# A two-layer gated cross-attention and mixture kernel: two of four probability tiles turned by VectorE and transfers, and plain steps in another order

## The reference

```python
x = x + tanh(g_xattn[0]) * L0_xattn(layernorm(x), ctx)
x = x + tanh(g_ffn[0])   * L0_ffn(layernorm(x))       # linear layer with weights from 4 bit planes
x = x + tanh(g_xattn[1]) * L1_xattn(layernorm(x), ctx) # 16 heads of 128
x = x + tanh(g_ffn[1])   * L1_ffn(layernorm(x))       # 16 experts, top 4, first batch's 512 rows only
...
q = rmsnorm(hidden @ Wq, gq); k = rmsnorm(enc @ Wk, gk); v = enc @ Wv
attn = softmax(q @ k.T * scale)
out  = (attn @ v) @ Wo
```

## Time and profile before

| | us |
|---|---|
| median of 3 runs | 1463.31 |
| fastest and slowest run | 1462.25, 1465.47 |
| span of the profiled execution | 1461.5 |
| PE busy | 1437.8 |
| DVE busy | 1107.0 |
| ACT busy | 977.5 |
| POOL busy | 864.5 |

### The profile page before, as it was taken

The page is one execution under the profiler, slowest core; times in us unless marked ns, Lnnn a source line. Parts: engine busy times, 40 slices in busy tenths (PEclk is TensorE's granted clock), DMA queues, the critical chain, the costliest instruction groups (busy, mean ns, idle before and its releaser), DMA issues.

```text
span 1461.5 us, 23763 instructions
## 1 busy us (share of the span) xinstructions
PE 1437.8 (98%) x8086; PEld 1223.0 (84%) x8086; DVE 1107.0 (76%) x2100; ACT 977.5 (67%) x2224; POOL 864.5 (59%) x701
## 2 busy tenths in 40 slices
PE   8999999999999999999999999999999999999998
PEld 6778788888888888888888888888888888888887
DVE  7888777777777777777777777777777776787777
ACT  7864477777776667667676767667676765666664
POOL 4785555555554566666575757575666655664341
PEclk9999999999999999999999999999999999999999
DMA  8420011111111333434333433433434331321002
GB/s 325 159 66 16 22 44 45 57 44 44 44 44 44 139 124 126 149 108 147 124 129 127 139 123 127 139 117 132 136 115 144 125 126 36 107 82 37 8 1 87
DMA packets 55495, 142.74 MB, mean 98 GB/s; under 512 B 5392, under 2 KB 5392, under 8 KB 55376
## 3 DMA queue, kind: packets, MB, share of 16 engines
q1 hardware_dynamic: 51616, 128.90, 26.1%
q0 software_dynamic: 3760, 12.32, 3.0%
HBM read 126.79 MB, written 14.42 MB: 97 GB/s over the span
## 4 chain that ended last, share of the span: by engine, by line
PE 82%; DVE 7%; ACT 4%; POOL 4%; issue 2%; DMA 0%; ACTq 0%; SPq 0%; DVEq 0%; POOLq 0%
PE w_bank L505 10%; PE w_bank L507 10%; PE w_bank L506 10%; PE j_bank L505 9%; PE j_bank L507 9%; PE j_bank L506 9%; PE t_bank L573 7%; PE s_bank L505 4%; PE s_bank L507 4%; PE s_bank L506 4%; PE t_bank L538 2%; POOL q_scale L1855 2%; POOL wo_lo L1815 2%; ACT prob L927 1%; PE t_bank L657 1%
## 5 line engine op out<-in xcount | busy, mean ns | idle before, releaser
L927 ACT ACTIVATE prob<-s_bank,neg_bias,q_scale 128x512 f32<-128x512 f32 x255 | 198.0, 777 | 186.5 <-DVE neg_bias L1422 186.4
L1262 DVE TENSOR_TENSOR probT_lo<-t_bank,probT_hi 128x512 fp32r<-128x512 f32 x260 | 176.4, 689 | 168.4 <-ACT probT_hi L892 168.4
L1476 DVE SCALAR_TENSOR_TENSOR x_sb<-w_bank,inv_sum,x_sb 128x512 f32<-128x512 f32 x254 | 188.4, 744 | 0.0
L1401 DVE TENSOR_REDUCE neg_max<-s_bank 128x1 f32<-128x512 f32 x255 | 168.6, 682 | 0.9 <-PE s_bank L507 0.9
L1815 POOL TENSOR_TENSOR xnT_lo<-xnT_raw,xnT_hi 128x512 fp32r<-128x512 f32 (+2 forms) x47 | 126.5, 2693 | 61.5 <-ACT xnT_hi L892 61.5
L573 PE MATMUL t_bank<-ident,prob 128*128 128x128 f32 x1008 | 151.4, 273 | 1.3 <-ACT prob L927 1.1
L892 ACT CAST probT_hi<-t_bank 128x512 fp32r<-128x512 f32 x260 | 150.1, 590 | 1.8 <-PE t_bank L515 1.8
L1855 POOL TENSOR_TENSOR q_scale<-q_ss,minus_half 128x4 f32<-128x4 f32 x64 | 65.9, 1030 | 143.6 <-DVE q_ss L1414 143.6
L505 PE MATMUL j_bank<-wkv_lo,cT_hi 128*128 128x256 f32 x512 | 145.1, 283 | 0.7 <-DVE oT_lo L1262 0.4
L507 PE MATMUL j_bank<-wkv_hi,cT_lo 128*128 128x256 f32 x512 | 144.6, 282 | 0.0
L506 PE MATMUL j_bank<-wkv_hi,cT_hi 128*128 128x256 f32 x512 | 144.4, 282 | 0.0
(11 more groups left out here) (308 smaller groups left out, 4454.2 us busy)
## 6 DMA issues: line engine op xcount, KB each, us to landing
stage<-w SPq DMA_DIRECT2D x96, 256.0 KB, 3.4
xnT_raw<-w_gu SPq DMA_DIRECT2D x31, 704.0 KB, 4.8
cT_raw<-w_gu SPq DMA_DIRECT2D x31, 704.0 KB, 4.7
xnT_raw<-w_dn SPq DMA_DIRECT2D x16, 768.0 KB, 4.4
cT_raw<-w_dn SPq DMA_DIRECT2D x15, 768.0 KB, 4.7
planes<-bits SPq DMA_DIRECT2D x16, 512.0 KB, 4.8
y<-stage SPq DMA_DIRECT2D x31, 256.0 KB, 4.0
x_sb<-x SPq DMA_DIRECT2D x5, 1024.0 KB, 10.9
```

What stands on the lines that cost most here:

```text
L927: nc.scalar.activation(prob[:, i, :], score_bank(t, i)[:], ACT.Exp, bias=neg_bias[:, u % 2, i:i + 1], scale=q_scale[:, u % 2, i:i + 1], ac ...
L1262: return nc.vector.tensor_tensor(dst, src, hi, ALU.subtract)
L1401: nc.vector.tensor_reduce(neg_max[:, u % 2, i:i + 1], score_bank(t, i)[:], AX_X, ALU.max, negate=True).then_inc(own_max, 1)
L1476: nc.vector.scalar_tensor_tensor(out=here, in0=w_bank[0][:] if packed else out_bank(t, i)[:], scalar=inv_sum[:, w % 2, i:i + 1], in1=here, ...
```

## The change

In 53 steps two of the four tiles (0 and 1, "the pair") are no longer turned by PE. `moved(u)` says for which items: steps 3 to 62 but 19 and 52 to 57, that is the 31 packed steps and 22 plain ones (3 to 18, 51, 58 to 62). There

- ACT's exponential writes the pair with the keys in another order in the row (32 at a time);
- DVE turns each 32x32 square of the pair's 128x1024 numbers in place (`turn_quads`);
- SP stores the pair, 512 KB, to a buffer `turn` in device memory (`store_pair`), waits until that has landed, and loads it back with the squares in their new partitions by four transfers of 128 KB whose pieces are 512 bytes (`load_pair`);
- ACT copies the pair's high part and POOL lowers its low part, as one 128x1024 instruction each (`moved_hi`, `moved_lo`). In packed steps both stand at the end of the same step, in plain steps at the start of the next.

ACT may overwrite the pair's tiles in `prob` only after `moved_lo` (`pair_lo`), and `values` waits for it too. All four tiles are now stored in `probT` in the pair's order of queries, and the value product reads and writes through views of 32.

Plain steps have a new order on every engine, in the steps that are not moved (2, 19, 52 to 57) too: on PE the value product comes after the key and value projections and goes to a bank of its own, both probability turns 0 and 1 come after an output projection; the key and value weights of a new head are split one step early on ACT and POOL (`next_wkv`). On SP the weights of a step now come ahead of the pair's transfers, and in packed steps the load of the down weights stands between the pair's store and its loads.

```diff
+def moved(u):
+    return 3 <= u + 1 < NI - 1 and u + 1 != T0 - 1 and not T0 + NB < u + 1 < T0 + NB + 7
...
+def turned_tiles(u):
+    return (2, 3) if moved(u) else range(NT)
...
+            def store_pair(u):
+                if not moved(u):
+                    return
+                sp.wait_ge(p_quads, MOVES[u] + 1)
+                wait(sp, p_moved, 16 * NT * MOVES[u])
+                sp.dma_start(turn_dram.rearrange("i p m -> p i m"), prob_pair).then_inc(p_stored, 16)
+            def load_pair(u):
+                if not moved(u):
+                    return
+                sp.wait_ge(p_stored, 16 * (MOVES[u] + 1))
+                for c in range(NT):
+                    sp.dma_start(prob[c * QUAD:(c + 1) * QUAD, 0:2, :].rearrange("a i (r m) -> a (i r) m", r=NT),
+                                 turn_dram.rearrange("i (r a) (c m) -> c a (i r) m", r=NT, c=NT)[c]).then_inc(p_moved, 16)
...
+                if in_block(t):
+                    store_pair(t - 1)
+                    down_weights(b, e)
+                    load_pair(t - 1)
...
+                if not in_block(t):
+                    store_pair(t - 1)
+                    load_pair(t - 1)
...
                 def probs(i):
+                    if i not in turned_tiles(u):
+                        return
...
+                    wait(pe, pair_lo, MOVES[w + 1])          # values()
...
+                if not packed:
+                    project_down()
+                    key_value(0, (0,))
+                    query_squares()
+                    key_value(0, (1,))
+                    late_turn()
+                    key_value(1)
+                    values()
...
+                    scores(2)
+                    scores(3)
+                    query((0, 1))
+                    project_out(0)
+                    probs(0)
+                    project_out(1)
+                    probs(1)
+                    probs(2)
+                    query((2, 3))
+                    key_turn()
+                    project_out(2)
+                    probs(3)
+                    project_out(3)
+                    return
...
+                    else:                                     # ACT, softmax(i) of the pair
+                        wait(act, pair_lo, MOVES[u])
...
+                def moved_hi(v):
+                    act.wait_ge(p_moved, 16 * NT * (MOVES[v] + 1))
+                    copy_hi(probT_pair(0), prob_pair).then_inc(pair_hi, 1)
...
                 late_norm()
+                if not in_block(t - 1):
+                    moved_hi(w)
...
+                    inner_hi()
+                    moved_hi(u)
+                    query_squares()
...
+                def turn_quads():                             # DVE
+                    need(dve, p_exp, 4, u, 2)
+                    flat_pair = prob_pair.rearrange("p i s -> p (i s)")
+                    nc.vector.transpose(flat_pair, flat_pair).then_inc(p_quads, 1)
...
+                add(0)                                        # DVE, plain step
+                add(1)
+                values_rows()
...
+                take(1)
+                probs_lo(0)
+                probs_lo(1)
+                probs_lo(2)
...
+                def moved_lo(v):                              # POOL
+                    pool.wait_ge(pair_hi, MOVES[v] + 1)
+                    lower(probT_pair(1), prob_pair, f32(probT_pair(0))).then_inc(pair_lo, 1)
...
+                if not in_block(t - 1):
+                    moved_lo(w)
                 query_scale()
...
                 down_lo()
+                if in_block(t):
+                    moved_lo(u)
                 if t != NI - 1:
                     squares_lo()
```

341 lines of the change are left out of this document (180 added, 161 removed).

## The result

The changed kernel takes 1493.91 us (median of 4 runs, 1489.41 to 1494.45), the kernel before 1464.39 in the runs beside it. The ratio is 1.0197, with an interval from 1.0183 to 1.0211: slower by 2%. I had forecast 1450, faster, and a range up to 1486. The profiled execution has a span of 1492.2, which is 30.7 above the 1461.5 of before.

A forecast was written before the change was run, and what follows sets the result against it. PE, busy 98% of the span, was taken to set the pace. Moved plain steps -22, unmoved +11, packed -2 sum to -13: span 1461.5 to 1448.5, median 1450; own range 1438 to 1460, wider range 1416 to 1486.

The forecast's parts named there:

- Plain steps with the pair moved: 22 plain steps: PE's saving shortens them until the loop sets the pace; -22 us together, -12.2 of it in steps 3 to 15.
- the loop of 16.65: Steps 3 to 15: copy, lowering, q_scale, exponentials and round trip take 15.75, with weight loads 16.65 us, setting the step's length.
- the sign that I had given: Plain steps: ACT waiting longer than 1 us for a DMA ahead of its 128x1024 copy would show the slower rival.
- the slower rival: Round trip too long, in plain steps' loop and packed steps' down weights behind the store: +24 us, 1487; chance 0.24.
- The new operations: Prices of the moved work: DVE's turn 1.15, ACT's copy 1.05, POOL's lowering 2.4, store 3.7, loads 4.1 us.
- the whole round trip: From DVE's turn through store and four loads to landed data: 9.2 us, in packed steps up to 1 more.
- Packed steps: 31 steps: a PE saving of 0.88 against a mean wait of 0.8, so -0.1 a step, -2 us in all.
- PE waits 0.5: Packed steps: POOL lowers the pair first, so the squares are ready at 4.5, where PE wants them at 4.05 us.
- hidden by 0.4 us only: Packed steps: down weights land at about 18.1, ACT's copy ends at 19.6, and POOL wants it at 20.0 us.
- Steps not moved: Eight plain steps lose by the new order: +1.0 each, +1.75 with a take, +11 us together.
- The third turn's wait: Unmoved plain steps: PE waits about 1.5 us at turn 2, which needs DVE's late low part of turn 0.
- the 0.5 a step (4 us) that was to go: Unmoved plain steps: 0.5 us of small PE waits that go, set against the third turn's wait.

The follow-up runs named there:

- the swap: VectorE takes the sums of squares out of the bank ahead of its 128x1408 low part in packed steps, against the kernel with the three edits: 1467.98 us.
- the three edits: Changed kernel with down weights ahead of the pair's store, squares ahead of the pair, and low parts of tiles 0 and 1 early in plain steps: 1476.39 us.
- the values experiment: Half the key and value projection ahead of the values product on TensorE in packed steps, against the kernel with the three edits and the swap: 1472.83 us.
- The low parts early: Changed kernel with VectorE lowering probability tiles 0 and 1 directly behind additions 0 and 1 in plain steps, ScalarE's high parts ahead of next_wkv: 1483.00 us.
- the kernel with more squares: The kernel before the change, with GpSimd lowering the squares three times instead of once in packed steps: 1585.81 us, ratio 1.0829.

## Why the prediction was wrong

- **Plain steps with the pair moved: the mechanism was right, the size nearly.** -17.1 against -22. The undisturbed step is 16.26, which is PE's own 16.2 of the prediction, below the loop of 16.65. But the loop is hardly shorter: in most of steps 3 to 16 ScalarE's copy starts 0.02 behind the landing. So any delay of the pair lengthens the step. In four steps (6, 10, 11 and 15) ScalarE waits 1.1 to 2.8 for it, and the step or the next comes out 1 to 4 us longer; in three of the four the store itself takes 5.0 to 5.9, in the fourth it is issued 0.95 later than elsewhere. That is the sign that I had given for the slower rival, in 4 of 22 steps. In the fifteen kernels whose steps 3 to 15 are the same program but for the place of the next head's split and of a `take`, these 13 steps took 213 to 219 us; which ones are long changes from kernel to kernel.
- **The new operations were priced right.** The turn 1.245 (1.15 predicted), ScalarE's copy 1.06 (1.05), GpSimd's low part 2.41 (2.4), the whole round trip 9.5 in plain steps and 9.9 in packed ones (9.2, and up to 1 more behind the down weights). By the figure of the Trainium skill, "VectorE: DVE Perf Modes", section "The three transpose paths", the turn would have been an estimated 2.5 us. The trace has half of that, and the measurement decides. In packed steps the pair landed 0.6 to 2.8 ahead of ScalarE's copy, much as I had said (1 to 2). The slower rival's conditions (a turn of 2.4, loads of 6) did not come, though one of the places that it names did: the down weights behind the store. That its 1487 is near the measured time is luck.
- **Packed steps: the step that failed.** I wrote "PE waits 0.5", 1.4 in every third, and set it against a saving of 0.88. In this sum TensorE waits in one place only, for `sqs_lo`, and each other piece of the engines keeps its old price. That one wait was taken too large (0.8 a step, 24 us in the window above, where it is 14.6; the 1.65 at which the pair starts in every third step is 1.4 by the earlier trace rows, 0.11 + 1.3, and its wait 1.1). Four terms were missing. The down weights, "hidden by 0.4 us only", were not hidden: their landing grew by 1 us, ScalarE waits 33 us, and TensorE 18.8 and 16.6 for `h_row` and the additions behind them. Pieces of GpSimd and VectorE that run beside each other do not keep their price: 2.65 for 1.30, and VectorE's 1408 at 2.0 in the mean of the packed steps for 1.67. The delay goes on through VectorE to `q_ss` and the exponentials, which the swap of two VectorE instructions showed (8.6 us). And the views and the early split cost 5.1 with no pair at all. With the three edits and the swap the pair in packed steps still costs 740.4 - 733.1 = 7.3, where 27 were to be saved. (The 733.1 are without the swap, but there the 1408 piece is at 1.62 and the gather at 1.05 anyway.) The rows behind the values experiment show where the 27 go: the step no longer follows TensorE's work but the chain through VectorE, ScalarE and GpSimd to the turn of the keys, and by these rows the pair's copy on ScalarE is a part of what lengthens it. Of the 20.4 us for the pair, 13.1 are order and 7.3 stay in every order that I tried.
- **Steps not moved: right in kind, half the size.** +20.8 for the eight against +11. The third turn's wait was priced right: 1.5, and 2.25 with a `take`, where the trace shows 1.43 or 1.44 in steps 2, 19, 52 and 53 and 2.10 to 2.46 in 54 to 57, 14.9 in all against 15 (step 63, which I had left out, has one of 1.43 too). One of them:

```profile
1346.02 1.09 PE L641 MATMUL t_bank<-ident,prob 128*128 128x128 f32 x4 [2.46 <-DVE probT_lo L1370]
```

  What failed is what I set against it and beside it: the 0.5 a step (4 us) that was to go did not show, the clock fell at two of these waits (3.4 us), and two waits for GpSimd's query weights (`wq_lo`, 1.4) came in. The low parts early give back 8.1 of the 20.8, some 2.5 of it by the clock, moving the pair there as well about as much again.
- The total: 17.1 saved, 25.5 + 20.8 + 1.5 lost. Of the price of the new waits, the clock is 6.8.

What stays open: how much of a packed step comes back if VectorE's chain to the exponentials is shortened, which no run tried, and why the store takes 5 to 6 us in single plain steps and 4 in their neighbours. Putting the store ahead of the weights on the queue did not mend it.

## What to carry to other kernels

Work that is moved off the bounding engine is priced on every engine that takes a part of it, and along the chain to the next thing for which the bounding engine waits: here 0.88 us of TensorE were free to remove in plain steps and cost more than they saved in packed ones, so the version to keep moves the pair in all plain steps and in no packed one (1452.1). When two waits feed on each other, mending one of them can be slower than mending none; test them together before dropping a theory. And a step order laid out for one case (two turns) should be checked on the steps that don't have it.

## What the runs showed of the hardware

- A VectorE instruction with two SBUF operands and a GpSimd instruction over SBUF hold each other up: 128x512 on GpSimd 2.65 instead of 1.30, 128x1408 on VectorE 2.53 instead of 1.62, a row gather issued by GpSimd 2.26 instead of 1.05, GpSimd's `q_scale` of 128x4 1.95 instead of 1.05. Both directions occur. A swap in the order moves them to other pieces, here to one that nothing waited for. The kernel before had them too, where they cost nothing that shows: its 1408 takes 1.67 in the mean and its gather 1.44.
- A VectorE scaling of 128x4 with one tensor operand (`inv_sum`) takes 0.9 to 1.1 beside GpSimd's 128x512 low part and ends with it (744.83 and 744.80 in the rows shown), 0.23 without it.
- Beside a wait of about 2 us TensorE's granted clock can fall to its lower level for a few us. It did at 1.99 in one packed step, and at the like waits of three others of the same kernel (1.94, 2.24 and 1.87; steps of 25.93 to 25.97) it did not. In the kernel with more squares 26 of 31 such waits had it (2.25 to 2.29, one of 3.5), and 44 us came from it. So two profiles of the same steps can differ by 1.6 us a fall.
- VectorE turns the squares of 128x1024 floats in 1.245 us, 1.244 to 1.249 in all 53 pieces.
- The same twelve matmuls take 0.12 us longer where their moving side and their bank are seen through views of 32 columns (0.71 instead of 0.68 for each of the four groups).
